# First layer of a two-layer graph network: the exponential blocks of a half's last chunk are summed on GpSimd too, and its denominators come from the sums

## The chip, the cores and the metric

One core of one Trainium2 chip runs the whole kernel in one launch. The metric is the device time of an execution in microseconds (us); lower is better. Engines are named as in the profile: PE is TensorE (PEld its weight loads), DVE is VectorE, ACT is ScalarE, POOL is GpSimd, SP is SyncE, whose queue issues the DMAs.

## The reference

Two layers follow each other on x (8 batches, 2048 nodes, 256 features) with one adjacency matrix (2048 x 2048). Only the first is touched here. Its attention takes a softmax within each chunk of 256 keys, so every query row has one denominator per head and chunk:

```python
h = relu(layernorm(x))
q, k, v = (h @ W.T + b, split into 4 heads of 64)      # per head
scores = clip(q . k / 8, -10, 10); where adj == 0: -10 # 8 chunks of 256 keys
attn   = softmax(scores, over the 256 keys of a chunk)
ctx    = sum over the 8 chunks of attn @ v
x      = x + layernorm(ctx @ Wo.T + bo + h) * gamma + beta
```

The second layer is a graph attention on the result, and its code is the same in both kernels.

## The kernel before, in words

**Tiling.** The first layer goes through the 8 batches one after another, each batch through 4 tiles of 512 query columns, each tile through two **halves** of 4 chunks. A chunk has 256 keys (2 blocks of 128) and 4 heads (2 pairs), which makes two **groups**, one for each pair; a group is 2 blocks of `e_sb`, each 128 keys x 2 heads x 512 queries. So a half has 8 groups, g0 to g7, and 4 chunks, c0 to c3 (chunk c is made of g2c and g2c+1). All four engines run the same loop over **steps** k = 0 to 63 of a batch, one group a step, with 9 further steps between two batches (projections of the next batch). Below, *phase* is k modulo 8, so that group gi has its scores at phase i. The order of the work is written out by hand: in each step an engine asks a few tables of offsets what is due.

**A step.** PE writes the scores of the group into PSUM (L815, tile `psS`). DVE clips and masks them into `e_sb` (L684, twice a step), ACT takes the exponential in place (L583, twice a step). One step later PE multiplies the two blocks with v into `psN` (L828, "numerators"), and one step after that ACT copies them out to one of 13 slots of `num` (L521). `e_sb` has 8 slots, so four groups.

**Denominators.** For chunks c0, c1 and c2, POOL adds the two key blocks of each group, one step after the scores, into `e_sum` (L414 in `sum_blocks`, 128x1024 fp32, 3 slots); I call these sums **s0** to **s7** after their groups. `SUMMED = GPH - PAIRS` = 6 of them exist before. PE then multiplies the two sums of a chunk with a matrix of ones and zeros, which puts the four heads' denominators into rows of `psD` (L847 in `denominators`; 4 matmuls, 8 instructions in the trace, for each chunk), at the end of phases 3, 5 and 7. The last chunk c3 has no sums: PE takes both key blocks straight from `e_sb` (L841; 8 matmuls, 16 instructions), at the end of the next phase 0. PE's wait in the code is `esum_done` for L847 and none for L841.

**After a half.** ACT reads `psD` (L530, next phase 2), DVE inverts it in four pieces (L697, phases 2 and 3), ACT and DVE split it into two parts `r_s` (L537 and L704, phase 4), and from phase 5 on PE spreads the inverse rows with a small matmul into `psM`, group by group (L861), DVE multiplies them into `num` (L659), and POOL adds the product to the context `ctxT` (L427 for the first two of a tile, L431 after that). I call these adds **a0** to **a7**, after the group of the half that has just ended. POOL does a0 at phase 6, a1 and a2 at 7, a3 at 0, a4 and a5 at 1, a6 at 2, a7 at 3; the first half of a tile has only a2 to a7. In a step POOL does its adds first, then the sum, then small rsqrt work (L101 to L107, L442 to L453) and the affine of a finished tile (L460, L465, L470, L474, 128x1024 each). After a7 of a tile's second half PE projects the context (L875, phases 3 and 4).

**Who waits for POOL's adds.** ACT's copy into a slot of `num` waits until POOL has added what stood there (`ctx_done`). PE's L875 waits for the last add of a tile. The rsqrt for the next batch is at steps 54 to 57, that is around the half boundary k = 56; for a finished tile it is at phases 7, 0 and 1 of the boundaries k = 32, 48 and 64.

Of the kernel before, what the change touches and what calls it, by code (L numbers as in the profile page):

```python
# [28 lines left out]
PAIRS = H // 2  # L29
# [16 lines left out]
CPH = CH // 2  # L46
BSTEPS = T * STEPS
GPH = CPH * PAIRS
# [72 lines left out]
def layer0(nc, mask, x, adjT, wqT, wkT, wvT, woT, bq, bk, bv, bo, gamma, beta, x1, nb):  # L121

    with ExitStack() as ctx:
# [120 lines left out]
            i = g % (2 * GPH)  # L244
            return g // (2 * GPH) * (2 * GPH - PAIRS) + (i + 1 if i < PAIRS else i + 1 - PAIRS)

        SUMMED = GPH - PAIRS

        def sum_of(n):

            h, i = divmod(n, GPH)
            return h * SUMMED + i if i < SUMMED else None

# [101 lines left out]
        def _(pool):  # L357
# [46 lines left out]
            def sum_blocks(b, g):  # L404
# [6 lines left out]
                if q >= SUMS:  # L411
                    h, i = divmod(q - SUMS, SUMMED)
                    pool.wait_ge(sums_done, h * CPH + i // PAIRS + 1)
# [342 lines left out]
        def _(pe):  # L756
# [76 lines left out]
            def denominators(b, ch):  # L833
                c, n = ch % CPH, b * (GROUPS // PAIRS) + ch
                if c == 0 and n >= CPH:
                    pe.wait_ge(sums_read, n // CPH)
                q = sum_of(PAIRS * n)
                if q is None:
                    for kb in range(KPC):
                        for hd in range(H):  # L840
                            ins = pe.matmul(psD[32 * hd:32 * hd + 32, :], hot[:, c, :],  # L841
                                            e_sb[:, (SPC * n + KPC * (hd // 2) + kb) % ES, hd % 2, :],
                                            start=False, stop=kb == KPC - 1, skip_group_check=True)
                else:
                    pe.wait_ge(esum_done, q + PAIRS)
                    for hd in range(H):
                        ins = pe.matmul(psD[32 * hd:32 * hd + 32, :], hot[:, c, :], e_sum[:, (q + hd // 2) % SUMS, hd % 2, :],  # L847
                                        start=c == 0, stop=False, skip_group_check=True)
                ins.then_inc(sums_done, 1)

            def broadcast(b, half, i):
# [33 lines left out]
            for b in range(nb):  # L885
                for k in groups_of(b):
                    if k == GROUPS and b + 1 < nb:
                        turn(b + 1, 0, False)
                    for bb, kk in alive(b, k):
                        for half, i in picked(kk, 0):  # L890
                            broadcast(bb, half, i)
                    if k < GROUPS:
                        scores(b, 2 * k)
                        scores(b, 2 * k + 1)
                    for bb, kk in alive(b, k):
                        for half, i in picked(kk, 1):
                            broadcast(bb, half, i)
                    if 1 <= k <= GROUPS:
                        numerators(b, k - 1)
                    if k % 2 and 3 <= k < GROUPS + 2 and sum_of(k - 3) is not None:  # L900
                        denominators(b, (k - 3) // 2)
                    if k % 2 == 0 and 2 <= k <= GROUPS and sum_of(k - 2) is None:
                        denominators(b, (k - 2) // 2)
                    for bb, kk in alive(b, k):
                        project(bb, kk)
                    if b + 1 < nb:
                        for v in (2 * (k - GROUPS), 2 * (k - GROUPS) + 1):
                            prepare(b + 1, v, False)
# [553 lines left out]
def build(nc, x, adjT, wqT, wkT, wvT, woT, bq, bk, bv, bo, gamma, beta, w, a1, a2, out):  # L1462
    x1 = nc.dram_tensor("x_between", [NB, N, F], F32).ap()

    with nc.sbuf_tensor("mask", [P, BLK, N], I8) as mask:
        layer0(nc, mask, x, adjT, wqT, wkT, wvT, woT, bq, bk, bv, bo, gamma, beta, x1, NB)
        layer1(nc, mask, x1, w, a1, a2, out, NB)
# [27 lines left out]
```

## Time and profile before

| | |
|---|---|
| median of 3 runs | 4598.11 us (4597.84 to 4601.86) |
| profiled execution | 4597.83 us |
| its span | 4596.0 us |
| PE busy | 4386.1 us (95%) |
| POOL busy | 3009.0 us (65%) |
| L841, denominators of c3, PE | 121.6 us, 1024 instructions |
| L847, denominators of c0 to c2, PE | 200.1 us, 1536 instructions |
| L414, sums on POOL | 918.5 us, 384 instructions |
| granted TensorE clock, mean | 0.983 |

The span is the time from the first to the last instruction of the profiled execution; its own time is 1.8 us longer. The first layer fills the span up to about 2920 us, the second the rest. The page's busy times are sums over both layers, so how an engine stands in the first layer has to be read from its own stretches.

### The profile page before, as it was taken

How to read it: one execution, taken by the hardware profiler on the slowest of the kernel's cores; microseconds unless marked ns; L12 is line 12 of the kernel's file. 1: busy time of each engine (PE TensorE's matmuls, PEld its weight loads, DVE VectorE, ACT ScalarE, POOL GpSimd, SP SyncE). 2: the span in 40 equal slices, each digit the busy share in tenths (PEclk: the TensorE clock that was granted, in tenths of full speed). 3: DMA queues.
4: the chain of work that ended last, by engine and by line, in shares of the span. 5: the costliest groups of instructions: out<-in, count | busy, mean ns of one | idle time of the engine just before them, and what ended most of it. 6: DMA issues, size and time to landing. Idle time of an engine off the chain costs nothing. (4 is left out here: it accounts for less than half of the span.)

```text
span 4596.0 us, 84237 instructions
## 1 busy us (share of the span) xinstructions
PE 4386.1 (95%) x34312; PEld 2615.8 (57%) x34312; DVE 3494.4 (76%) x4562; ACT 2987.9 (65%) x3498; POOL 3009.0 (65%) x2422
## 2 busy tenths in 40 slices
PE   7999999999999999999999999389999999999997
PEld 3334334334334334333333433279999999999997
DVE  5875775775776776776687577478898989889895
ACT  4664664664665565556466466188887888888885
POOL 5685685675775676577477477356665757667585
PEclk9999999999999999999999999689999999999999
DMA  6001000000001000001000000111121212112011
GB/s 197 10 10 37 10 10 28 19 10 28 19 10 28 19 10 28 10 10 33 15 10 19 10 10 19 35 47 50 56 68 41 75 32 70 54 47 82 29 59 42
DMA packets 126979, 160.88 MB, mean 35 GB/s; under 512 B 8832, under 2 KB 109184, under 8 KB 126592
## 3 DMA queue, kind: packets, MB, share of 16 engines
q1 hardware_dynamic: 126592, 155.49, 10.7%
q8 instruction: 271, 4.44, 0.4%
q14 instruction: 116, 0.95, 0.1%
HBM read 121.64 MB, written 33.83 MB: 34 GB/s over the span
## 5 line engine op out<-in xcount | busy, mean ns | idle before, releaser
L583 ACT ACTIVATE e_sb<-e_sb 128x1024 f32<-128x1024 f32 x1024 | 1082.4, 1058 | 835.7 <-DVE e_sb L684 798.3
L684 DVE SCALAR_TENSOR_TENSOR e_sb<-psS,mask 128x1024 f32<-128x1024 f32 x1024 | 1202.9, 1216 | 348.0 <-PE psS L815 341.5
L1414 PE MATMUL psA<-xy,ring_p 128*128 128x195 bf16 x8192 | 1405.1, 248 | 13.6 <-DVE red L1294 13.6
L1414 PE MATMUL psA<-xy,ring_s 128*128 128x195 bf16 x8192 | 1404.6, 249 | 0.0
L414 POOL TENSOR_TENSOR e_sum<-e_sb 128x1024 f32<-128x1024 f32 x384 | 918.5, 2392 | 325.5 <-ACT e_sb L583 219.0
L1214 ACT ACTIVATE ring_s<-eiB,ejb 128x1024 int8<-128x1024 f32 x1024 | 1089.8, 1137 | 9.5 <-PE psA L1414 9.5
L815 PE MATMUL psS<-qT,kT 64*128 64x512 f32 x4096 | 1042.2, 613 | 3.0 <-DVE e_sb L684 2.9
L828 PE MATMUL psN<-e_sb,v_sb 128*32 128x512 f32 x8192 | 985.0, 598 | 0.0
L1414 PEld LDWEIGHTS psA<-xy,ring_p 128*128 128x128 fp8e4 x8192 | 801.5, 98 | 19.9 <-DVE red L1294 17.0
L1414 PEld LDWEIGHTS psA<-xy,ring_s 128*128 128x128 fp8e4 x8192 | 800.5, 98 | 8.6 <-issue 0.3
L431 POOL TENSOR_TENSOR ctxT<-ctxT,num 128x512 f32<-128x512 f32 x384 | 488.1, 1277 | 456.2 <-DVE num L659 349.9
L815 PEld LDWEIGHTS psS<-qT,kT 64*128 64x128 f32 x4096 | 407.0, 186 | 519.6 <-issue 269.1
L828 PEld LDWEIGHTS psN<-e_sb,v_sb 128*32 128x32 f32 x8192 | 213.6, 109 | 621.3 <-issue 617.0
L659 DVE TENSOR_TENSOR num<-num,psM 128x512 f32<-128x512 f32 x512 | 348.9, 681 | 272.1 <-PE psM L861 251.0
L1152 POOL TENSOR_TENSOR red<-red,cq 128x260 f32<-128x260 f32 x256 | 367.1, 1453 | 241.5 <-DVE red L1294 241.5
L1286 DVE TENSOR_TENSOR ring_p<-mask,ring_s 128x1024 int32<-128x1024 int32 x256 | 456.1, 1782 | 8.8
L861 PE MATMUL psM<-r_s,pick 64*128 64x512 f32 x512 | 347.0, 678 | 34.0 <-DVE num L659 23.4
L1284 DVE TENSOR_TENSOR ring_s<-ring_s,mask 128x1024 int32<-128x1024 int32 x256 | 344.9, 1347 | 43.1 <-ACT ring_s L1214 41.6
L521 ACT ACTIVATE num<-psN 128x512 f32<-128x512 f32 x512 | 298.3, 583 | 103.8 <-POOL ctxT L427 62.4
L1294 DVE TENSOR_REDUCE red<-psA 128x130 f32<-128x390 f32 x512 | 269.7, 556 | 115.2 <-PE psA L1414 97.1
L1165 POOL TENSOR_TENSOR o_sb<-red,rden 128x256 f32<-128x256 f32 x128 | 115.4, 902 | 272.7 <-DVE rden L1299 271.9
L760 PE MATMUL psS<-hT,w_s 128*128 128x512 f32 x512 | 235.0, 602 | 21.0 <-ACT hT L508 12.8
(120 smaller groups left out, 4158.0 us busy)
## 6 DMA issues: line engine op xcount, KB each, us to landing
eiB<-ei_between SPq DMA_DIRECT2D x64, 512.0 KB, 4.1
xin<-x SPq DMA_DIRECT2D x32, 512.0 KB, 3.9
xr<-x SPq DMA_DIRECT2D x32, 512.0 KB, 4.8
x_between<-hy SPq DMA_DIRECT2D x32, 512.0 KB, 3.2
xin<-x_between SPq DMA_DIRECT2D x32, 512.0 KB, 5.6
xo<-x_between SPq DMA_DIRECT2D x32, 512.0 KB, 4.5
out<-o_sb SPq DMA_DIRECT2D x32, 512.0 KB, 5.3
xr<-adjT SPq DMA_DIRECT2D x24, 512.0 KB, 4.1
```

Source lines behind the costliest of these rows:

```text
L414: pool.tensor_tensor(e_sum[:, q % SUMS], e_sb[:, KPC * n % ES], e_sb[:, (KPC * n + 1) % ES], ALU.add)\
L431: pool.tensor_tensor(ctxT[:, pair, :], ctxT[:, pair, :], num[:, n % NS, :], ALU.add)\
L583: act.activation(e_sb[:, n % ES], e_sb[:, n % ES], ACT.Exp, scale=SCALE).then_inc(exp_done, 1)
L659: dve.tensor_tensor(num[:, n % NS, :], num[:, n % NS, :], psM[:, :], ALU.mult).then_inc(norm_done, 1)
L684: dve.scalar_tensor_tensor(out=e_sb[:, n % ES], in0=psS[:, s % 2], scalar=-CLIP_RAW, in1=mask[:, kb, cols][:, None, :].to_broadcast([P, 2, ...
L815: ins = pe.matmul(psS[:, s % 2, i, :], kT[rows, pair, kb * P:(kb + 1) * P], qT[rows, pair, t * TW:(t + 1) * TW], start=True, stop=True)
L828: ins = pe.matmul(psN[32 * part:32 * part + 32, pair, :], v_sb[:, kb, col:col + 32], e_sb[:, n % ES, i, :], start=u % KPC == 0, stop=u % K ...
L861: pe.matmul(psM[:, :], pick[rows, i, :], r_s[rows, :], start=True, stop=True).then_inc(bcast_done, 1)
L1152: ins = pool.tensor_tensor(r[:, :, br, :], r[:, :, br, :], cq[:, b % 2, br, blocks, hd][:, :, None].to_broadcast([P, TB, XW]), ALU.mult)
L1214: ins = act.activation(ring_s[:, n % RING, k, :], eiB[:, V % 2, :], ACT.Sign, bias=ejb[:, b % 2, KC * c + k, hd:hd + 1])
L1286: dve.tensor_tensor(pos_w[:, r], edges, neg_w[:, r], ALU.bitwise_xor).then_inc(pos_done, 1)
L1414: ins = pe.matmul(psA[:, i % BANKS, br * PARTS * XW:(br + 1) * PARTS * XW], part[:, n % RING, k, tt * TW + j * P:tt * TW + (j + 1) * P], x ...
```

## The change

`SUMMED` becomes 8: `sum_of` now gives every group a sum. POOL adds two more pairs of blocks in each half, s6 at phase 7 and s7 at phase 0 of the next half. The branch L841 is no longer reached; c3 goes the way of the other chunks (4 matmuls with a wait for `esum_done`), and by the rule "k odd, two steps after the chunk" it moves from the end of phase 0 to the end of phase 1. DVE's clips, which waited for c3's denominators before they overwrote its blocks, now wait for the sums. Numbers of lines after the first edit are 2 lower in the changed kernel.

```diff
-
-
-        SUMMED = GPH - PAIRS
+        SUMMED = GPH
 
         def sum_of(n):
...
                     pe.wait_ge(esum_done, q + PAIRS)
                     for hd in range(H):
                         ins = pe.matmul(psD[32 * hd:32 * hd + 32, :], hot[:, c, :], e_sum[:, (q + hd // 2) % SUMS, hd % 2, :],
-                                        start=c == 0, stop=False, skip_group_check=True)
+                                        start=c == 0, stop=c == CPH - 1, skip_group_check=True)
```

**Place 1: PE at the half boundary k = 56 of the first batch.** The rows run from the numerators of g6 (phase 7) to the scores of phase 2. Before:

```order
141 L828 MATMUL psN<-e_sb,v_sb 32x512 x8
142 L847 MATMUL psD<-e_sum,hot 32x512 x4
143 L861 MATMUL psM<-r_s,pick 128x512
144 L815 MATMUL psS<-qT,kT 128x512 x4
145 L861 MATMUL psM<-r_s,pick 128x512
146 L828 MATMUL psN<-e_sb,v_sb 32x512 x8
147 L841 MATMUL psD<-e_sb,hot 32x512 x8
148 L815 MATMUL psS<-qT,kT 128x512 x4
149 L861 MATMUL psM<-r_s,pick 128x512
150 L828 MATMUL psN<-e_sb,v_sb 32x512 x8
151 L815 MATMUL psS<-qT,kT 128x512 x4
```

Now:

```order
141 L826 MATMUL psN<-e_sb,v_sb 32x512 x8
142 L845 MATMUL psD<-e_sum,hot 32x512 x4
143 L859 MATMUL psM<-r_s,pick 128x512
144 L813 MATMUL psS<-qT,kT 128x512 x4
145 L859 MATMUL psM<-r_s,pick 128x512
146 L826 MATMUL psN<-e_sb,v_sb 32x512 x8
147 L813 MATMUL psS<-qT,kT 128x512 x4
148 L859 MATMUL psM<-r_s,pick 128x512
149 L826 MATMUL psN<-e_sb,v_sb 32x512 x8
150 L845 MATMUL psD<-e_sum,hot 32x512 x4
151 L813 MATMUL psS<-qT,kT 128x512 x4
```

The 8 matmuls of c3 at the end of phase 0 are gone, and 4 stand one step later, behind the numerators of the next half's g0.

**Place 2: POOL at the same boundary**, from a1 and a2 of phase 7 to a6 of phase 2. Before:

```order
143 L431 TENSOR_TENSOR ctxT<-ctxT,num 128x512 x2
144 L104 TENSOR_TENSOR tmp<-rs 128x16
...
148 L431 TENSOR_TENSOR ctxT<-ctxT,num 128x512
149 L104 TENSOR_TENSOR tmp<-rs 128x16
...
153 L431 TENSOR_TENSOR ctxT<-ctxT,num 128x512 x2
154 L414 TENSOR_TENSOR e_sum<-e_sb 128x1024
155 L104 TENSOR_TENSOR tmp<-rs 128x16
...
161 L431 TENSOR_TENSOR ctxT<-ctxT,num 128x512
```

Now:

```order
162 L429 TENSOR_TENSOR ctxT<-ctxT,num 128x512 x2
163 L412 TENSOR_TENSOR e_sum<-e_sb 128x1024
164 L104 TENSOR_TENSOR tmp<-rs 128x16
...
168 L429 TENSOR_TENSOR ctxT<-ctxT,num 128x512
169 L412 TENSOR_TENSOR e_sum<-e_sb 128x1024
170 L104 TENSOR_TENSOR tmp<-rs 128x16
...
174 L429 TENSOR_TENSOR ctxT<-ctxT,num 128x512 x2
175 L412 TENSOR_TENSOR e_sum<-e_sb 128x1024
176 L104 TENSOR_TENSOR tmp<-rs 128x16
...
182 L429 TENSOR_TENSOR ctxT<-ctxT,num 128x512
```

Two sums (L412) are inserted, s6 ahead of the rsqrt part of phase 7 and s7 ahead of that of phase 0; all that follows on POOL stands behind them.

## Rows read from the trace of the kernel before

**Rows 1.** Busy time by engine in one batch period, and in the second layer.

```profile
core 0: us, PE busy (x) PEld busy (x) DVE busy (x) ACT busy (x) POOL busy (x), PEclk, DMA share, GB/s
954.20:1311.90 357.70, 352.55 (x2144) 136.14 (x2144) 257.74 (x326) 207.35 (x269) 238.59 (x201) 1.00 0.06 19
2940.00:4596.00 1656.00, 1557.56 (x17153) 1521.42 (x17152) 1402.21 (x1883) 1323.22 (x1352) 1060.20 (x736) 0.97 0.16 53
```

**Rows 2.** Groups of instructions by line, whole run: busy us, mean ns, idle before.

```profile
L847 PE MATMUL psD<-e_sum,hot 128*32 128x512 f32 x1536 | 200.1, 593 | 6.5 <-POOL e_sum L414 6.5
L841 PE MATMUL psD<-e_sb,hot 128*32 128x512 f32 x1024 | 121.6, 592 | 0.0
L414 POOL TENSOR_TENSOR e_sum<-e_sb 128x1024 f32<-128x1024 f32 x384 | 918.5, 2392 | 325.5 <-ACT e_sb L583 219.0 <-PE psD L847 82.4 <-issue 22.7
```

**Rows 3.** Timeline of PE, k = 55 to 60 of a batch: start, duration, line.

```profile
1037.34 1.99 PE L815 MATMUL psS<-qT,kT 64*128 64x512 f32 x8
...
1041.22 1.04 PE L847 MATMUL psD<-e_sum,hot 128*32 128x512 f32 x8
...
1042.20 1.98 PE L815 MATMUL psS<-qT,kT 64*128 64x512 f32 x7
...
1046.09 1.90 PE L841 MATMUL psD<-e_sb,hot 128*32 128x512 f32 x16
1047.92 1.99 PE L815 MATMUL psS<-qT,kT 64*128 64x512 f32 x8
...
1051.92 1.99 PE L815 MATMUL psS<-qT,kT 64*128 64x512 f32 x8
...
1059.58 1.04 PE L847 MATMUL psD<-e_sum,hot 128*32 128x512 f32 x8
1060.56 1.99 PE L875 MATMUL psM<-w_o,ctxT 128*128 128x256 f32 x8
```

**Rows 4.** Timeline of POOL at the tile boundary k = 48.

```profile
1001.56 1.27 POOL L427 TENSOR_TENSOR ctxT<-num 128x512 f32<-128x512 f32 x1 [1.92 <-DVE num L659]
...
1005.40 1.27 POOL L427 TENSOR_TENSOR ctxT<-num 128x512 f32<-128x512 f32 x1 [0.85 <-POOL rs L107]
...
1019.92 1.27 POOL L431 TENSOR_TENSOR ctxT<-ctxT,num 128x512 f32<-128x512 f32 x1 [0.38 <-DVE num L659]
```

**Rows 5.** Timeline of ACT at the same place: copies of numerators and exponentials.

```profile
1006.76 0.60 ACT L521 ACTIVATE num<-psN 128x512 f32<-128x512 f32 x1 [1.00 <-POOL ctxT L427]
1008.66 2.19 ACT L583 ACTIVATE e_sb<-e_sb 128x1024 f32<-128x1024 f32 x2 [1.30 <-DVE e_sb L684]
```

**Rows 6.** Timeline of POOL around k = 56, with the next batch's rsqrt.

```profile
1034.80 1.28 POOL L431 TENSOR_TENSOR ctxT<-ctxT,num 128x512 f32<-128x512 f32 x1
1036.04 2.37 POOL L414 TENSOR_TENSOR e_sum<-e_sb 128x1024 f32<-128x1024 f32 x1
...
1047.97 2.35 POOL L414 TENSOR_TENSOR e_sum<-e_sb 128x1024 f32<-128x1024 f32 x1
1050.29 0.21 POOL L104 TENSOR_TENSOR tmp<-rs 128x16 f32<-128x16 f32 x1
...
1052.23 1.27 POOL L431 TENSOR_TENSOR ctxT<-ctxT,num 128x512 f32<-128x512 f32 x1 [0.18 <-DVE num L659]
1053.46 2.39 POOL L414 TENSOR_TENSOR e_sum<-e_sb 128x1024 f32<-128x1024 f32 x1
1056.22 1.27 POOL L431 TENSOR_TENSOR ctxT<-ctxT,num 128x512 f32<-128x512 f32 x1 [0.37 <-DVE num L659]
```

**Rows 7.** PE's waits for other engines in the first layer: us, times, longest.

```profile
PEld psM L861 <- DVE num L659: 106.3, 125, 1.1
PEld psM L861 <- DVE r_s L704: 17.4, 17, 1.1
PEld psD L847 <- POOL e_sum L414: 15.2, 15, 1.9
PE psD L847 <- POOL e_sum L414: 6.5, 7, 1.0
```

**Rows 8.** DVE's L704: durations ns min/median/max, and one in the timeline.

```profile
L704 DVE SCALAR_TENSOR_TENSOR r_s<-r_s,lo_rows,r_f x64: 742/744/2492, 124.6 to 2882.4; 128x512 fp32r<-128x512 f32 x64
...
1027.79 2.36 DVE L704 SCALAR_TENSOR_TENSOR r_s<-r_s,lo_rows,r_f 128x512 fp32r<-128x512 f32 x1
```

## The prediction

> **What bounds the kernel now.** I began with busy times by stretch. In one batch period of the first layer PE is busy 352.55 of 357.70 us, DVE 257.74, POOL 238.59 and ACT 207.35 [rows 1]. PE's own work is the bound there at full clock (1.00), and only 5 us of a period are left as waits. The second layer is not touched and should keep its time, only shifted. So an instruction less on PE is worth its time as long as nobody makes PE wait for it; POOL has 119 us free per period, but freedom on average says nothing about the half boundaries, where the change puts its work. Next I looked at whom PE waits for. It already waits for POOL's sums once in most batches (7 waits, longest 1.0 us), and for `r_s` a few times [rows 7]. The gaps between starts on PE and POOL at the boundaries are in the timelines [rows 3, 4, 6], and the sum below is worked from those.
>
> **What PE saves.** The price of c3's denominators is read from step lengths, start of scores to start of scores. A step without denominators lasts 1051.92 - 1047.92 = 4.00 us, one with 4 matmuls (L847) 1042.20 - 1037.34 = 4.86, the one with 8 (L841) 1047.92 - 1042.20 = 5.72 [rows 3]. So 4 matmuls cost 0.86 and 8 cost 1.72. The change swaps 1.72 at phase 0 for 0.86 at phase 1: 0.86 us a half, and over 64 halves 55.0 us. The grouped rows agree: 121.6 us for L841 [rows 2], half of which is 60.8, a little above since overlapping ends are counted there; I take the step lengths. The moved denominators end at phase 1 and ACT reads `psD` at phase 2, behind its copy, so the read is not delayed.
>
> **What POOL has to add.** Two sums a half, 128 in all. Their span is 2.39 us in the mean [rows 2], but from the start of one to the start of what follows with no wait between is 2.32 us (1047.97 to 1050.29), and an add takes 1.24 (1034.80 to 1036.04) [rows 6]. A queue that runs back to back advances by these spacings, so I count 2.33 and 1.24. The Trainium skill, Perfetto Trace Analysis, GPSIMD Engine Instruction, says to time GpSimd by start-to-start spacing and not by the reported span. With the spans of these rows (2.39 and 1.27) the loss worked out next would be 3.4 us instead of 2.5 and the sum 6 us higher.
>
> **Tile boundary k = 48 (likewise 16, 32, 64).** Here the rows show gaps that the sums can use. a2 starts at 1001.56 and a3 only at 1005.40 [rows 4], between them 1.65 us of rsqrt. New: a2 to 1002.80, s6 to 1005.13, rsqrt to 1006.8, a3 to 1008.05, s7 to 1010.4. PE wants s7 for c3 at the end of phase 1, at about 1013.7 (old step start 1005.90, now 4.0 us steps): not waited for. Then rsqrt, a4, a5, s0, rsqrt, a6 and s1 follow back to back and end at 1021.6; PE wants s1 for c0 at 1022.4 (0.86 earlier than now). Covered with 0.8 us to spare. a7, now started at 1019.92 [rows 4], starts at 1021.6. **Who is queued behind a3:** ACT's copy into `num` waits for it even now (1.00 us, starting at 1006.76), and the exponentials of the step stand behind the copy and begin at 1008.66 [rows 5]. The copy would start at about 1008.1 and end at 1008.7: the exponentials move by 0.1 us or less, and PE, which wants them at 1011.9, now leaves 1.0 us of slack where it had 2.9. No cost.
>
> **Half boundaries k = 24 and 40.** Same count from the rows there: at k = 24 POOL is back to back from a0 to a4 already, and PE waits 0.9 us for s5. That wait hangs on a7 of the tile before, which itself comes 0.86 us earlier, so it stays as it is. Behind it s7 ends about 0.2 us before PE wants it, s1 about 0.25 before. At k = 40 there is 1.5 us. No cost, but k = 24 has no reserve.
>
> **Half boundary k = 56.** Here the next batch's rsqrt (about 4.7 us in four parts) stands in the same steps. POOL comes in with little slack: a0 at 1034.80 follows without a wait, and a6 at 1052.23 and a7 at 1056.22 waited only 0.18 and 0.37 us for DVE [rows 6]. With the sums: a0 at 1034.9, s5 to 1038.5, rsqrt and a1, a2 to 1041.6, s6 to 1043.9, rsqrt and a3 to 1046.4, s7 to 1048.7, rsqrt and a4, a5 to 1052.4, s0 to 1054.7, rsqrt to 1056.5, a6 to 1057.7, s1 to 1060.0, a7 to 1061.3. PE wants s7 at 1049.1 (fine) and s1 for c0 at 1057.7: now it starts there at 1059.58 [rows 3], and would be 1.72 us plus rounding earlier. It waits 2.3 us plus the signal, and then 0.3 us more for a7 ahead of L875. Its next scores start 2.5 us after where the full gain would put them. The seven batches that have a successor pay this: 17.5 us. Bounds: nothing, if the queue is faster than I count; 3.4 us each by the spans, 24 us.
>
> **The other places.** Between two batches (k = 64 to 72) PE's steps are long, and s7 is done several us before PE is at c3. k = 8 has no adds, so POOL is free. At the end of the layer the inverse chain is at most 1 us better or worse. POOL's sums remove c3's wait from DVE's clips and put one four steps back in its place: nothing.
>
> **Sum.** 55.0 - 17.5 = 37.5 us. The profiled execution took 4597.8 (0.3 below the median), so **4560 us**.
>
> **Rivals.**
>
> *POOL keeps up everywhere.* If the chain at k = 56 is 2.5 us shorter than counted, the whole 55 us stay: 4543. For it: DVE's `num` products come earlier, too. Against: the chain has no idle to give but the 0.18 and 0.37 us of the rows [rows 6]. 15%.
>
> *`r_s` comes late.* L704 takes 0.74 us as a rule and up to 2.49 [rows 8]; the long ones, such as the 2.36 us at 1027.79, fall on running POOL instructions, and PE's broadcast waited 0.2 us right behind it [rows 7]. With more work on POOL, it may meet one more often. If it waits for a whole sum at the 24 tile boundaries within batches, it ends 2.33 + 0.74 us after 1026.9, at 1030.0, and PE, ready at 1029.1, loses its 0.86 us there: 24 x 0.86 = 21 us, 4581. In my order s3 ends at about 1027.5, so L704 would come a little earlier than now instead. The Trainium skill, SBUF — State Buffer, Who interferes with whom, says that a DVE instruction with two SBUF inputs and a GpSimd one that reads SBUF lock each other out, whole instructions at a time; L704 reads `r_s` and `r_f`. By that rule, moving work to GpSimd is not free for DVE; the rows with 2.36 us agree. 12%.
>
> *Slower: POOL becomes the pace at every boundary.* The mechanism is the wait for `esum_done` at c3 and c0. My margins are 0.2 to 1.5 us after chains of a dozen POOL instructions. Were each 0.17 us longer than its spacing (a signal to be waited for in each, an add held by DVE), the chain would be 2 us late. PE would wait about 1.3 us at 48 boundaries (k = 16 to 56 of 8 batches), 62 us: 4622. It turns slower than before from 0.8 us of new wait per boundary (37.5 / 48). Against it: such signals are in the spacings counted. 8%.
>
> *No change.* PE's saved time could reappear as waits for exponentials or clips, since steps at the boundary get shorter (5.72 to 4.00 us). DVE has 100 us free per period and ACT 150 [rows 1], and the slack worked out above is 1.0 us, so I don't expect it: about 4598. Or the change is not what it says: the order of the instructions shows the 4 matmuls gone, so this is only the risk that their 0.86 us were hidden. 8% together.
>
> **How the numbers follow.** Forecast 57%, own range 4550 to 4572. The range that should hold 8 in 10 reaches from the full gain, 4541, to the late `r_s` with both bounds of k = 56, 4592. A measurement of this kernel can tell 0.2% (9 us) from no change. Faster by more: forecast, full gain, late `r_s`, 0.84 less a little, 0.85 with what of the others falls below 4589; within 0.2%: 0.08; slower: 0.07.
>
> **What would show it.** The batch period should fall from 357.7 to about 353.3 us (8 x 0.86 less 2.5). No L841; PE's step at phase 0 4.0 us, at phase 1 4.86 us. PE's waits for POOL's sums should gain one of about 2.3 us per batch at c0 behind k = 56, and a short one at L875. POOL should be busy about 300 us more in all. Waits of PE for sums at k = 16, 32, 40 or 48 would show the count of POOL's chain wrong; waits at L861 for `r_s` above 0.3 us the lock; a step at phase 0 still above 5 us the saving.

## The result, and the profile after

The changed kernel took 4573.01 us (median of 4 runs, 4571.85 to 4574.45), the one before 4599.98 us on the same occasions: a ratio of 0.9941 with a 95% interval of 0.9924 to 0.9959. It is 0.6% faster. The forecast was 4560 with a range of 4541 to 4592; the direction held, the size was 27 us in place of 38.

The page of the changed kernel, first its parts 1 and 2 (busy time, and the granted clock in tenths over 40 slices), then the group of the sums:

```profile
span 4572.7 us, 83469 instructions
...
PE 4340.3 (95%) x33800; PEld 2601.2 (57%) x33800; DVE 3475.3 (76%) x4562; ACT 2979.0 (65%) x3498; POOL 3300.2 (72%) x2550
...
PEclk9999999999999999999999999699999999999999
...
L412 POOL TENSOR_TENSOR e_sum<-e_sb 128x1024 f32<-128x1024 f32 x512 | 1214.6, 2376 | 226.1 <-ACT e_sb L581 103.2
```

PE has 512 instructions fewer, POOL 128 more and 291 us more work. One batch period, in the view of stretches that stands in [rows 1] for before:

```profile
938.00:1292.90 354.90, 347.37 (x2088) 134.73 (x2084) 255.62 (x326) 206.44 (x268) 275.03 (x217) 1.00 0.06 19
```

The period fell from 357.7 to 354.9 us, not to 353.3 as forecast. PE's busy time fell by 5.2 us to 347.4, though 6.9 us of matmuls were taken out, and what PE is not busy rose from 5.2 to 7.5 us. So there are two things to find: a wait that came, and matmuls that became longer. Both are in the timeline of PE around k = 56, which answers to [rows 3] (L845 are the denominators, L873 the projection, L813 the scores):

```profile
1031.47 1.98 PE L813 MATMUL psS<-qT,kT 64*128 64x512 f32 x7
...
1035.46 1.99 PE L813 MATMUL psS<-qT,kT 64*128 64x512 f32 x8
...
1039.79 1.06 PE L845 MATMUL psD<-e_sum,hot 128*32 128x512 f32 x8 [0.26 <-POOL e_sum L412]
1040.79 1.99 PE L813 MATMUL psS<-qT,kT 64*128 64x512 f32 x8
...
1044.79 1.99 PE L813 MATMUL psS<-qT,kT 64*128 64x512 f32 x8
...
1051.15 1.48 PE L845 MATMUL psD<-e_sum,hot 128*32 128x512 f32 x8 [2.52 <-POOL e_sum L412]
1052.56 3.22 PE L873 MATMUL psM<-w_o,ctxT 128*128 128x256 f32 x8
1055.72 1.13 PE L813 MATMUL psS<-qT,kT 64*128 64x512 f32 x4
```

The step at phase 0 is 35.46 - 31.47 = 3.99 us long (5.72 before): the saving is there. c3, one step later, waits 0.26 us for s7, and c0 waits 2.52 us for s1. Behind that wait the same 8 instructions of L845 take 1052.56 - 1051.15 = 1.41 us where they took 0.98 before [rows 3], and the 8 of L873 take until 1055.72, 3.16 us where the same 8 take 1.92 in the trace of before (L875, 1060.56 to 1062.48). The view of stretches gives TensorE's granted clock (the number behind the engines' times) during the wait and in these two groups:

```profile
1048.70:1051.10 2.40, 0.00 (x0) 0.00 (x0) 1.86 (x3) 2.40 (x5) 2.40 (x3) 1.00 0.00 0
1051.15:1052.56 1.41, 1.41 (x8) 0.16 (x8) 0.00 (x0) 1.41 (x3) 1.41 (x2) 0.69 0.00 0
1052.56:1055.70 3.14, 3.14 (x11) 2.35 (x8) 0.00 (x0) 2.35 (x5) 3.14 (x2) 0.60 0.00 0
```

PE was idle for 2.5 us, of which the first row shows 2.4, and right behind that it ran for most of the next four at 1.2 GHz instead of 2.4 (means of 0.69 and 0.60). In the trace of before there is no such fall in the first layer's attention, in this one there are seven, one per batch that has a successor, each beginning 0.4 to 0.7 us after the start of c0's denominators at this place.

POOL's queue at that place, which answers to [rows 6] (the rsqrt instructions, 0.2 to 0.3 us each and back to back, are left out):

```profile
1036.12 1.27 POOL L429 TENSOR_TENSOR ctxT<-ctxT,num 128x512 f32<-128x512 f32 x1
1037.35 2.38 POOL L412 TENSOR_TENSOR e_sum<-e_sb 128x1024 f32<-128x1024 f32 x1
...
1040.89 2.50 POOL L429 TENSOR_TENSOR ctxT<-ctxT,num 128x512 f32<-128x512 f32 x2
1043.34 2.39 POOL L412 TENSOR_TENSOR e_sum<-e_sb 128x1024 f32<-128x1024 f32 x1
...
1047.42 1.28 POOL L429 TENSOR_TENSOR ctxT<-ctxT,num 128x512 f32<-128x512 f32 x1
1048.65 2.35 POOL L412 TENSOR_TENSOR e_sum<-e_sb 128x1024 f32<-128x1024 f32 x1
1050.96 1.28 POOL L429 TENSOR_TENSOR ctxT<-ctxT,num 128x512 f32<-128x512 f32 x1
```

No instruction here waited for another engine; s1, started at 1048.65, ends at 1051.00, and PE starts at 1051.15. It is the queue's length that PE waits for.

### The profile page after: what moved, and what is told of

Its sections match the earlier page's. It is cut to its first block and busy times, and to the rows that moved or that the text cites. A ratio compares the mean times of both kernels' runs of the same rounds, so it can differ in the third digit from the quotient of the medians.

```text
span 4572.7 us, 83469 instructions
## 1 busy us (share of the span) xinstructions
PE 4340.3 (95%) x33800; PEld 2601.2 (57%) x33800; DVE 3475.3 (76%) x4562; ACT 2979.0 (65%) x3498; POOL 3300.2 (72%) x2550
## 5 line engine op out<-in xcount | busy, mean ns | idle before, releaser
L412 POOL TENSOR_TENSOR e_sum<-e_sb 128x1024 f32<-128x1024 f32 x512 | 1214.6, 2376 | 226.1 <-ACT e_sb L581 103.2
L813 PE MATMUL psS<-qT,kT 64*128 64x512 f32 x4096 | 1042.3, 613 | 3.0 <-DVE e_sb L682 2.9
L813 PEld LDWEIGHTS psS<-qT,kT 64*128 64x128 f32 x4096 | 406.9, 186 | 519.7 <-issue 269.1
L845 PE MATMUL psD<-e_sum,hot 128*32 128x512 f32 x2048 | 269.9, 598 | 26.7 <-POOL e_sum L412 26.7
```

The source lines that it names most:

```text
L412: pool.tensor_tensor(e_sum[:, q % SUMS], e_sb[:, KPC * n % ES], e_sb[:, (KPC * n + 1) % ES], ALU.add)\
L813: ins = pe.matmul(psS[:, s % 2, i, :], kT[rows, pair, kb * P:(kb + 1) * P], qT[rows, pair, t * TW:(t + 1) * TW], start=True, stop=True)
```

## The experiments

The theory after this reading: the full gain is some 55 us; it is paid back at one place only, by POOL's queue around k = 56 (about 2.5 us per batch) and by TensorE's lower clock behind the wait that the queue makes (about 1.7 us per batch). The rivals: the added sums slow the layer in more places; the saving itself is smaller than it looks; the slow matmuls have another cause than the clock.

### e1: the rsqrt out of the way

```diff
-XSTATS_AT, RSQRT_AT, TURN_AT = (6, 8, 22, 24), (54, 55, 56, 57), (58, 59, 60, 61)
+XSTATS_AT, RSQRT_AT, TURN_AT = (6, 8, 22, 24), (43, 44, 45, 46), (58, 59, 60, 61)
```

> The changed kernel with the rsqrt of the next batch's norms moved from steps 54 to 57 to steps 43 to 46 on GpSimd. Theory (queue and clock): the changed kernel loses its time at one place, the half boundary k = 56 of seven batches, where GpSimd's queue is late by about 2.5 us and TensorE's granted clock then falls to 0.5 for 3.4 us (1.7 us more). With the rsqrt out of the way PE waits for no sum there, the clock stays at 1.00, the batch period falls from 354.9 to 350 to 351 us and the time to 4540 to 4545. Rival (the sums slow the whole layer, by lock or queue, at every boundary): the period stays above 353 and the time above 4560.

Measured: 4539.94 us, ratio to before 0.987 (0.9856 to 0.9883). One period:

```profile
923.30:1273.60 350.30, 345.53 (x2083) 133.92 (x2081) 256.83 (x326) 206.11 (x268) 275.49 (x217) 1.00 0.06 19
```

and PE behind k = 56:

```profile
1038.35 1.04 PE L845 MATMUL psD<-e_sum,hot 128*32 128x512 f32 x8
1039.33 1.99 PE L873 MATMUL psM<-w_o,ctxT 128*128 128x256 f32 x8
1041.25 1.99 PE L813 MATMUL psS<-qT,kT 64*128 64x512 f32 x8
```

No wait, the old 0.98 and 1.92 us. POOL does the same 217 instructions a period as in the changed kernel (275.5 and 275.0 us), only in another order, and the period is 4.6 us shorter. The rival of a slowdown everywhere falls.

### e2: the same move without the change

The same line in the kernel before.

> The kernel before with the same move of the rsqrt alone, as a control. Theory: before the change nobody waited for that rsqrt, so 4598 +- 3. Rival (the rsqrt at k = 54 to 57 costs something of its own, by holding DVE or ACT): 10 us or more faster, and then the gain of the experiment with both is not due to the sums.

Measured: 4600.72 us, ratio 1.0002 (0.9993 to 1.0011), period 357.7. The place of the rsqrt is worth nothing before the change and 33 us after it. What e1 gains over the changed kernel is thus the collision of the rsqrt with the new sums.

### e3: TensorE's part alone

```diff
-                    pool.wait_ge(sums_done, h * CPH + i // PAIRS + 1)
+                    pool.wait_ge(sums_done, h * CPH + (i // PAIRS + 1 if i < SUMMED - PAIRS else CPH))
...
                 if q is None:
-                    for kb in range(KPC):
...
+                    q = sum_of(PAIRS * (n - 1))
+                    for hd in range(H):
+                        ins = pe.matmul(psD[32 * hd:32 * hd + 32, :], hot[:, c, :], e_sum[:, (q + hd // 2) % SUMS, hd % 2, :],
+                                        start=False, stop=True, skip_group_check=True)
...
```

POOL makes no s6 and s7 here, and c3's 4 matmuls read the sums of the chunk before, so c3's denominators are wrong; only the time is of use. The lines behind the last dots move c3's denominators to the end of phase 1.

> TensorE's part alone: the last chunk's denominators are 4 matmuls at the end of phase 1 that read the sums of the chunk before, and GpSimd makes no sums s6 and s7 (so the last chunk's denominators are those of another chunk). Theory: 0.86 us less a half, and nothing to pay: 4598 - 55 = 4543, period 350.8, PE's step at phase 0 4.00 us. Rival (the saved time comes back as other waits of PE): clearly above 4550.

Measured: 4545.65 us (one run), period 351.0. The timeline of PE at k = 56: the step at phase 1 (with 8 instructions of denominators) is 1033.86 - 1029.01 = 4.85 us long, read as in [rows 3]:

```profile
1029.01 1.99 PE L815 MATMUL psS<-qT,kT 64*128 64x512 f32 x8
...
1032.89 1.04 PE L841 MATMUL psD<-e_sum,hot 128*32 128x512 f32 x8
1033.86 1.99 PE L815 MATMUL psS<-qT,kT 64*128 64x512 f32 x8
```

The step without them is 4.00 us (1033.86 to 1037.86 in the same trace). So the 0.86 us a half are real, and e1, with all of POOL's new work in it, is no slower than this kernel, which has none of it: it is 5.7 us faster, for a reason that is told below. The rival of a smaller saving falls.

### e4: GpSimd's part alone

`SUMMED = GPH`, but c3 keeps its place and its 8 matmuls from `e_sb`, and DVE's clips wait for them again:

```diff
-        SUMMED = GPH - PAIRS
+        SUMMED = GPH
...
+                        if q % GPH >= GPH - PAIRS:
+                            dve.wait_ge(sums_done, (n - ES) // SPC + 1)
...
-                if q is None:
+                if c == CPH - 1:
...
```

The lines behind the last dots keep c3's denominators at the end of phase 0.

> GpSimd's part alone: s6 and s7 are made, but the last chunk's denominators still come from the exponential blocks, 8 matmuls at the end of phase 0. Theory: PE comes to c0 behind k = 56 about 1.3 us later than in the changed kernel, so it waits some 1.3 us for s1 and 0.3 us for a7 in seven batches; as waits of 1.2 us elsewhere left the clock at 1.00, it stays there: 4598 + 12 = 4610. If the clock falls after the shorter wait, too: 4622. Rival (more sums cost DVE or ACT everywhere): waits at k = 16 to 48 as well, above 4625.

Measured: 4610.46 us (one run), period 359.2, against 4600.22 for the kernel before: 10 us slower, at no fall of the clock. PE behind k = 56:

```profile
1063.68 1.06 PE L849 MATMUL psD<-e_sum,hot 128*32 128x512 f32 x8 [0.44 <-POOL e_sum L414]
1064.84 1.99 PE L877 MATMUL psM<-w_o,ctxT 128*128 128x256 f32 x8
```

The cost per batch, 359.2 - 357.7 = 1.5 us, is near what I expected (1.3 and 0.3), but its parts are others. The step of k = 59 is 0.8 us longer than before: 0.6 by the wait at c0 (0.44 us of idle time in the view) and 0.2 by a7, for which L877 starts 1.16 us after c0's denominators and not 0.98. These are the two that I had at 1.3 and 0.3. The other 0.6 us stand where I had nothing: the steps k = 37 and 53, where PE waits for `r_s` behind a tile boundary, are 0.3 us longer each (at k = 53 5.64 us for 5.33 before), and PE's idle time for L706, the L704 of before, rose from 3.1 to 7.8 us in 16 waits (up to 2800 us of the span). So with POOL's part alone the rival of a late `r_s` does come true, at 0.6 us per batch. The run also shows that the change is worth doing only because PE's part is larger than what POOL's part costs.

### e5 and e6: the wait shortened in two doses

e5 moves only the first rsqrt part, `RSQRT_AT = (45, 55, 56, 57)`, e6 the first two, `(44, 45, 56, 57)`.

> The changed kernel with only the first of the four rsqrt parts (0.65 us of GpSimd) moved away, from step 54 to 45. Queue alone: the wait of 2.5 us behind k = 56 becomes 1.9 us, 7 x 0.65 = 4.5 us less: 4568.5. Queue and clock: the same if the clock still falls after 1.9 us; if it does not fall any more, another 12 us less, 4556.5. The traces so far show no fall after waits up to 1.3 us and one after 2.5, so this run may go either way.

> The changed kernel with the first two parts (1.8 us) moved to steps 44 and 45. Queue alone, with PE's slow stretch due to something other than the length of the wait: 7 x 1.8 = 12.6 us less, 4560. Queue and clock: the wait falls to about 0.7 us, the clock stays at 1.00 and the slow matmuls are gone, too, 12 us more: 4548.

Measured: e5 4563.92 us (ratio 0.9921, 0.9904 to 0.9937), e6 4548.39 us (0.9888, 0.9873 to 0.9903). In e6 the wait at c0 is 1.02 to 1.06 us (expected: 0.7), the clock is 1.00 throughout, and the time is the one that both causes together give; the queue alone would have left it at 4560. Both waits came out 0.3 us longer than expected (1.9 and 0.7), mainly because the wait at c3 disappears first and PE then comes to c0 sooner: in both runs the step behind phase 0 has its 4.85 us again (5.33 in the changed kernel). e5 turned out to be the better witness: the wait at c0 is 2.2 us in every batch, and the clock fell in five of the seven and not in the other two. One of each, PE's timeline with a fall:

```profile
339.76 1.76 PE L845 MATMUL psD<-e_sum,hot 128*32 128x512 f32 x8 [2.24 <-POOL e_sum L412]
341.45 2.94 PE L873 MATMUL psM<-w_o,ctxT 128*128 128x256 f32 x8
344.32 1.13 PE L813 MATMUL psS<-qT,kT 64*128 64x512 f32 x4
```

and without:

```profile
1048.14 1.06 PE L845 MATMUL psD<-e_sum,hot 128*32 128x512 f32 x8 [2.22 <-POOL e_sum L412]
1049.30 1.99 PE L873 MATMUL psM<-w_o,ctxT 128*128 128x256 f32 x8
1051.22 1.99 PE L813 MATMUL psS<-qT,kT 64*128 64x512 f32 x8
```

with their clocks, 0.55 and 1.00, in the view of stretches (the column behind POOL's busy time):

```profile
339.70:342.90 3.20, 3.14 (x12) 1.37 (x13) 0.00 (x0) 3.20 (x7) 3.20 (x2) 0.55 0.00 0
1048.10:1051.30 3.20, 3.07 (x18) 1.70 (x18) 0.00 (x0) 3.20 (x7) 3.20 (x2) 1.00 0.00 0
```

The same wait, the same code, one program: from c0's start to the next scores 4.56 us with the fall and 3.08 without. That is the price of the fall, 1.5 us. The other batches agree: the five with a fall take 4.45 to 4.71 us there, the two without 3.07 and 3.08. What decides between the two when the wait is 2.2 us long, no run shows.

### e7: the wait filled with useless matmuls

```diff
+                if ch == 28 and b + 1 < nb:
+                    for kb in range(KPC):
+                        for hd in range(H):
+                            pe.matmul(psD[32 * hd:32 * hd + 32, :], hot[:, c, :],
+                                      e_sb[:, (SPC * n + KPC * (hd // 2) + kb) % ES, hd % 2, :],
+                                      start=True, stop=True, skip_group_check=True)
```

> The changed kernel with 8 useless matmuls (1.7 us of TensorE work into psD, overwritten by the real ones) put in front of the wait for the sums at step 59 of seven batches. GpSimd and all waits for it are as in the changed kernel, so c0 starts at the same time. Clock theory: PE's idle stretch shrinks from 2.5 to about 0.8 us, the granted clock stays at 1.00, the matmuls behind it take their normal 0.97 and 1.92 us, and the kernel with more work is about 12 us faster, 4561. Rival (the slow matmuls come from the restart after a wait for a semaphore, or from weight loads, not from the clock): no change or up to 12 us slower, 4573 to 4585.

Measured: 4562.95 us (ratio to before 0.9917, 0.9903 to 0.9932), so 10 us faster than the changed kernel, with more work on TensorE. Its timeline (L838 are the useless matmuls):

```profile
1045.47 1.90 PE L838 MATMUL psD<-e_sb,hot 128*32 128x512 f32 x16
1048.10 1.07 PE L851 MATMUL psD<-e_sum,hot 128*32 128x512 f32 x8 [0.73 <-POOL e_sum L412]
1049.35 1.99 PE L879 MATMUL psM<-w_o,ctxT 128*128 128x256 f32 x8 [0.18 <-POOL ctxT L429]
1051.27 1.99 PE L813 MATMUL psS<-qT,kT 64*128 64x512 f32 x8
```

The idle stretch is 0.73 to 0.77 us, the clock does not fall, and the groups behind it have their usual lengths. POOL's queue was left alone, so this isolates the clock. It is 10 us and not the 12 expected for two reasons: the fall costs 1.5 us a time and not the 1.7 that I had put for it, and a wait for a7 that the slow matmuls had covered comes out (0.18 us in the view; from c0 to the next scores it is 3.17 us here and 3.08 in e5, so some 0.1 us a time). The Trainium skill, TensorE: Matmul & The Clock Gate, Part 1, has the rule behind it: the array's clock follows how busy it has recently been, 1.2 GHz after idling and 2.4 GHz after work. The runs agree, with 2.5 us of waiting enough here in seven of seven cases, 2.2 us in five of seven, and 1.2 us never; by that rule a forecast of a wait should always ask what the matmuls behind it will run at.

### e8: the last wait for a sum

In e1 PE's only wait for a sum is the old one at k = 23, but for one of 0.7 us at the end of the layer. Added to e1:

```diff
-YN_AT, AFFINE_AT = (19, 21), 28
+YN_AT, AFFINE_AT = (19, 21), 27
```

> The kernel of e1 (change and early rsqrt) with the affine of a finished tile one step earlier (offset 27 for 28), so that for the last tile of a batch it stands at steps 18 and 19 of the next batch and not at 19 and 20. PE's last wait for a sum, 0.9 us for s5 at k = 23 in seven batches, hangs on GpSimd being back to back from step 19 to 23. Theory: the 2.4 us that leave this stretch end the wait, 7 x 0.9 = 6 us off the 4540 of e1: 4534, period 349.4. Rival (the affine now makes a7 late and with it the whole chain behind it): the wait stays and the time is that of e1 or some us more.

Measured: 4535.15 us, ratio to before 0.9857 (0.984 to 0.9873); period 349.3:

```profile
943.90:1293.20 349.30, 345.45 (x2083) 134.00 (x2080) 257.39 (x326) 206.35 (x268) 275.82 (x217) 1.00 0.06 19
```

The wait at k = 23 is gone as forecast, with 5 us (6 expected; the step k = 21 in front of it became 0.2 us longer, and in the last batch the steps k = 45 and 61 half a microsecond each). This version beats both kernels, by 1.4% and 0.8%.

## Why the prediction was right, and where it was too large

**PE's saving: right.** 55.0 us forecast from two step lengths; e3, which has that saving and nothing else, is 54.6 us faster than the runs of before beside it (one run). Step by step it is 1.72 less 0.86 us at each half boundary within a batch, and 0.73 us in all at the one between batches. e1's period is 7.4 us shorter where 6.9 were forecast. What it has beyond e3 is at the places where PE waited 0.2 us for `r_s` behind tile boundaries: these waits disappeared (below), and the steps k = 37 and 53 are 0.46 us shorter each, against 0.2 us more at k = 51.

**POOL's queue: right by the instruction.** The count for k = 48 to 59 can be laid beside the trace, since k = 48 starts 9.40 us earlier there (996.50 for 1005.90):

| | forecast, shifted | measured |
|---|---|---|
| a3 starts, k = 48 | 997.4 | 997.57 |
| s7 ends | 1001.0 | 1001.20 |
| s1 ends, k = 50 | 1012.2 | 1012.32 |
| a0 starts, k = 54 | 1025.5 | 1025.77 |
| s7 ends, k = 56 | 1039.3 | 1039.73 |
| s1 ends, k = 58 | 1050.6 | 1051.00 |

The start-to-start spacings were the right unit: from a0 at k = 54 to the end of s1 they count 25.1 us, and the trace has 25.2. Most of the 0.4 us at the end was there before. No wait came up at k = 16, 32, 40 or 48, and the one of 0.9 us at k = 23 stayed as forecast (0.91). The copy on ACT that I had called queued behind a3 did wait 2.58 us, and the exponentials behind it cost nothing:

```profile
998.94 0.60 ACT L519 ACTIVATE num<-psN 128x512 f32<-128x512 f32 x1 [2.58 <-POOL ctxT L425]
999.44 2.00 ACT L581 ACTIVATE e_sb<-e_sb 128x1024 f32<-128x1024 f32 x2
```

**The step that failed: the price of the wait at k = 56.** I wrote that PE "waits 2.3 us plus the signal, and then 0.3 us more for a7", 2.5 us after the full gain, and bounded it by 0 and 3.4 us. Measured it is 354.9 - 350.3 = 4.6 us per batch, outside my bounds. Two things are in the difference:

- The queue's share is 3.2 us (353.5 in e7 less 350.3 in e1). The chain ended 0.4 us later than counted (the last two rows of the table), and PE started k = 56 at 1031.47, 0.5 us earlier than 1042.20 - 9.40 - 0.86 = 1031.94. So c3 waited 0.26 us where I had it "fine" by 0.4, and its step took 1040.79 - 35.46 = 5.33 us for 4.86, 0.5 more. c0 started 2.7 us late: 1051.15 for 1048.45, which is 1.74 us (1057.84 to 1059.58 in the trace of before) behind the numerators at 1046.71. This is the term that was mis-sized, by 0.7 us. A small part of it is the sum itself: 2.3 us, a signal and 0.3 us are at least 2.6, and I went on with 2.5.
- The clock's share is 1.4 us (354.9 less 353.5; 1.5 by e5's pair), and it was missing altogether. I priced a wait as its length and gave the matmuls behind it their old durations.

Over seven batches that is 15 us too little loss, against 4 us of gain that I had not counted (7.4 for 6.9 us in eight periods). So the gain should have been 37.5 - 14.7 + 4 = 26.8 us, and 27.0 were measured. The forecast of 4560 started from the profiled execution's 4597.8, and the runs of before have a median of 4600.0, which is the rest of the way to 4573.0. The time lies inside the wide range and 1 us above the forecast's own one of 4550 to 4572. That it came so near is in part luck: the 4 us of gain that I had not foreseen stood against the 15 us of loss that I had not.

**The rivals.** "POOL keeps up everywhere" is what e1 has made true; in the kernel as changed it did not. "`r_s` comes late" fell for the whole change, and with the sign turned: PE's waits for L704 in the first layer were 17.4 us in the weight-load row of [rows 7] and are 1.5 us now, though POOL is busier. The forecast expected L704 a little earlier, but counted no gain. It read their cost off as 0.2 us, a number that the rows it points to do not hold; by step lengths one costs 1033.34 - 1028.01 = 5.33 us for 4.86, that is 0.47 us. As with c3's 0.26 us above, a short wait of PE costs 0.2 to 0.3 us more than the idle time that the view gives for it. L702 (the old L704) at the tile boundary k = 52 took 1.25 us for 2.36 in [rows 8]:

```profile
1017.53 1.25 DVE L702 SCALAR_TENSOR_TENSOR r_s<-r_s,lo_rows,r_f 128x512 fp32r<-128x512 f32 x1
```

It comes up near the end of a POOL instruction now. Neither half of the change does this alone: in e3, with POOL's work as before, the waits are nearly those of before (17.3 us for 16.3 in the weight-load row up to 2800 us), and in e4, with the new sums and PE's work as before, they are longer (21.1 us). That where in a POOL instruction it falls counts, and not how busy POOL is, fits all of these, but is argued: no run moved L702 by itself. "POOL becomes the pace at every boundary" did not happen, nor did "no change". One remark of the forecast was wrong without a price: ACT's read of `psD` (L528) was delayed, 14 times and 7.8 us in all, and no step of PE became longer by it.

## What to carry to other kernels

A wait that a change adds on TensorE has two prices: its length, and the clock of the matmuls behind it; if it is long enough for the granted clock to fall, add what the next few microseconds of matmuls lose at half the rate (1.5 us here for each 2.5 us wait). Work handed to an engine that is a third idle has to be checked at the steps where it lands: here 36 us more per period cost nothing at any boundary but k = 56, and 4.6 us there, where it shared its steps with four small rsqrt parts, and moving those, worthless before, was worth more than the change had brought so far. To forecast such a queue, chain the start-to-start spacings of its own instructions through the new order and compare with the time at which the waiting engine arrives, itself shifted by what it has gained.

## What the runs showed of the hardware that I had not expected

- Adding 1.7 us of useless matmuls in front of a wait, seven times, made the kernel 10 us faster (e7).
- With the same wait of 2.2 us at the same place of the program the granted clock fell in five batches and stayed at 1.00 in two (e5), so that equal batches differ by 1.5 us. After waits of 1.2 us and less it never fell in the first layer's attention, after 2.5 us it fell in all seven.
